# Rotary halves by a DVE shuffle instead of extra products, the next step's transpose moved into the attention, and ACT empties turned banks ahead of the exponentials

## The chip, the cores and the metric

The program runs on one core of a Trainium2 chip. The metric is the time of one execution on the device in microseconds (us); lower is better. All data are float32.

## The reference, cut to what matters

A decoder on a batch of 4 sequences of 512 positions, width 128, with a context of 154 positions. Four groups of layers follow one another, with self attention, cross attention and feed-forward parts of different kinds. The change bears on the second group's four layers of rotary attention most:

```python
DEPTH, HEADS, DH, ROT = 4, 8, 64, 32
def apply_rope(t, freqs):
    t1, tp = (t[..., :rot], t[..., rot:])            # rot = 32 of the 64 features of a head
    rh = jnp.concatenate([-t1[..., d2:], t1[..., :d2]], axis=-1)   # d2 = 16
    t1 = t1 * jnp.cos(freqs) + rh * jnp.sin(freqs)
    return jnp.concatenate([t1, tp], axis=-1)
def attn_block(xq, ctx, Wq, Wk, Wv, Wo, bo, pe_q, pe_k, mask):
    q, k, v = heads(xq @ Wq), heads(ctx @ Wk), heads(ctx @ Wv)
    q, k = apply_rope(q * DH ** (-0.5), pe_q), apply_rope(k, pe_k)
    sim = jnp.einsum('bhid,bhjd->bhij', q, k)        # masked in the self attention
    out = jnp.einsum('bhij,bhjd->bhid', jax.nn.softmax(sim, axis=-1), v)
    return out @ Wo + bo
# a layer: x += attn(rms(x)); x += attn(rms(x), context); x += gelu(rms(x) @ W1 + b1) @ W2 + b2
```

## The kernel before

**Order of the work.** A loop runs twice, once for each pair of sequences; the two sequences of a pair are lanes A and B. `ORDER` lists the steps (kind 5 is rotary self attention, 6 rotary cross attention, 7 the feed-forward step; kinds 5, 6, 7 occur for four layers), and each step runs for lane A and then for lane B. So there are 16 rotary self steps and 16 rotary cross steps in one execution. Each engine (PE, ACT, DVE, POOL) has one instruction stream; the streams meet only in semaphores (`self.r...`). Besides its own work a step carries parts of its neighbours: `prev.tail` on DVE adds the output of the step before to X, `nxt.head` computes the root-mean-square norm of the step after (the other lane, so it doesn't depend on this step), with one `pow` on POOL, and `nxt.pe_head`/`nxt.act_head` transpose that step's normed X on PE into a PSUM bank `XB` (`ps_O1`) and copy it to `XT` on ACT.

**A rotary step** (`L1Attention`; `L1Cross` is the same class with the context's 154 keys) makes four chunks of two heads each for K and Q, transposed: features on the partitions, positions along the row. The 32-partition blocks of a chunk hold, for each of two heads, first the 32 rotated features and then the 32 plain ones; `sin` is zero on the plain ones and carries the minus sign. For each K or Q chunk (index j) PE makes two products: one with the weights (`wq`, `wk`), one with weights whose halves were exchanged on the host (`swapq`, `swapk`). They go round a ring of four PSUM banks (`RING`: P0, P1, O0, O1). DVE multiplies the one by `cos` into Q or K and the other by `sin` into `part` (in `wide`), and POOL adds the two (line 1526). `order` is K of all four chunks, then Q of all four. Then the attention starts. The values of V are made inside it, in step 1 (`fill`, `fill2`).

**The attention** (`Attention`, used by seven kinds of step). It proceeds in steps i. In step i PE makes the scores of round i (line 515, four banks: S0, S1, OUT, T; places k = 0..3), every so many rounds it transposes the spread reciprocals (line 528), then transposes the exponentials of round i-1 (line 546) into rotating banks `PP3` (P0, P1, O0; two banks in the step `L0Moe`), and multiplies the transposed probabilities of round i-2 by V (line 564). DVE takes maxima (line 662), or adds the mask and takes them (line 658), and ACT takes the exponentials (line 633). The transposed banks are emptied ("turned") into `wide`: places 0 and 3 by ACT (line 588), 1 and 2 by DVE (line 590); ACT also empties the bank of the reciprocals into `RS` (line 597). PE may write a bank only when its use three banks before has been emptied. The ACT stream of a step before the change is, for each place k: exponential (i, k), then after k = 0 the reciprocals, then turn (i-1, k). Without an added mask the scores of round i+1 at place k wait for the exponential (i, k), which read the bank; with an added mask they wait for DVE alone.

A rotary self step has 8 rounds (two a chunk), a rotary cross step 4 (one a chunk, two blocks of queries at each place). `project` (line 693) multiplies by Wo at the end.

Of the kernel before, what the change touches and what calls it, by code (L numbers as in the profile page):

```python
# [129 lines left out]
class Table:  # L130


    def __init__(self, rows, before=None):
# [4 lines left out]
        for r in rows:  # L138
            if r[3] == "A":
                a += 1  # L140
            else:
                d += 1
            self.count.append((r[3], a if r[3] == "A" else d))
# [20 lines left out]
class Step:  # L164
# [17 lines left out]

    def beside(self, dve, *which):
# [10 lines left out]
def build(nc, io):  # L194
    ctx = ExitStack()
    with ctx:
# [12 lines left out]
        consts = sb("consts", [P, nconsts])  # L209
        lora_bias = sb("lora_bias", [P, 4])  # L210
# [130 lines left out]

        def evacuate(eng, r, tab, who, lo=0, hi=None):
            for j, row in enumerate(tab.rows[lo:hi], lo):
                if row[3] != who:
                    continue
# [89 lines left out]
        class Attention:  # L435
# [3 lines left out]
            def __init__(self, heads, dh, nkeys, added=None, causal=False, keys=None, queries=None,  # L439
                         banks=None, split="ADDA", exes=None):  # L440
# [15 lines left out]
                self.seq, self.first = [], []  # L456
                done = {"A": 0, "D": 0}
                self.recip_at = []
                for rd in range(self.rounds + 1):
# [5 lines left out]
                    for k in range(4 if rd < self.rounds else 0):  # L465
                        done[split[k]] += 1
                        self.seq.append((split[k], done[split[k]]))

# [25 lines left out]
            def evacuated(self, eng, r, s):  # L494
                e, n = self.seq[s]
                eng.wait_ge(r.turned_act if e == "A" else r.turned_dve, n)

            def pe(self, pe, r, ready=(), beside=None, wo=None, fill=None, fill2=None, valued=()):
                nb = len(self.banks)
                for i in range(self.steps):  # L500
                    if i == 1 and fill:
                        fill(pe)
# [17 lines left out]
                    if i == 1 and fill2:  # L520
                        fill2(pe)
# [30 lines left out]
                    if 0 <= rd < self.rounds:  # L552
# [14 lines left out]
                        ins.then_inc(r.av, 1)  # L567
                    if beside:
# [41 lines left out]
            def pool(self, pool, r):  # L610
                for rd in range(self.rounds):
                    self.spread(pool, r, rd)

            def act(self, act, r, free=None, fill=None):
                for i in range(self.steps):
                    if i == 1 and fill:
                        fill(act)
                    for k in range(4):
                        if i < self.rounds:
# [17 lines left out]
                        if k == 0 and i >= 2 and (i - 1) % self.rpc == 0:  # L637
# [4 lines left out]
            def dve(self, dve, r, free=None, beside=None):  # L642
                for i in range(self.steps):
                    for k in range(4):
# [56 lines left out]
        class LaneStep(Step):  # L701
# [35 lines left out]
            def pe_head(self, pe):  # L737
# [11 lines left out]
            def act_head(self, act):  # L749
# [128 lines left out]
        class Store(Step):  # L878
# [14 lines left out]
            def pe_head(self, pe):  # L893
                pass

            def act_head(self, act):
# [587 lines left out]
        class L1Attention(RootMeanSquare):  # L1484
            cross = False
            kind = 5

            def __init__(self, *a):
# [10 lines left out]
                self.part = [wide[:, 2048 + SEQ * j:2048 + SEQ * (j + 1)] for j in range(4)]  # L1499
                values = [([(src[:, c * kc:(c + 1) * kc], w("wv"))], kc, SEQ, "A", "copy",  # L1500
                           v_rows(kc, 8, 64, 64, c), None) for c in range(nch)]
                self.tab = Table([row for j in range(8) for row in self.rotary(j)])
                self.values = Table(values, self.tab)

            def dest(self, m, c):
                return QT[:, c, :] if m == "q" else KT[:, c, 0:self.NK]

            def rotary(self, j):
                m, c = self.order[j]
                n = SEQ if m == "q" else self.NK  # L1510
                x = self.L.XT[:, :] if m == "q" else self.src[:, :]
                by = (lambda t: ("times", (0.125, t))) if m == "q" else (lambda t: ("row", (t, ALU.mult)))
# [946 lines left out]
```

## Time and profile before

| | |
|---|---|
| time, median of 3 runs | 4449.32 us (4441.46 to 4451.9) |
| the profiled execution's own time | 4439.93 us |
| its span, first to last instruction | 4437.0 us |
| PE busy | 4059.2 us, 91% |
| DVE busy | 2674.6 us, 60% |
| ACT busy | 1998.3 us, 45% |
| POOL busy | 861.7 us, 19% |
| mean granted TensorE clock | 0.982 |

The busy times are averages over very different stages; whether an engine bounds a stage is read from the order of time there. A float32 matmul shows as two records, so "x4" on line 339 is two products. Where operations are pipelined their spans overlap by some 0.1 us, so the time that one costs is from start to start.

### The profile page before, as it was taken

What the parts mean: (1) busy time and instruction counts of PE and PEld (TensorE: products, weight loads), DVE (VectorE), ACT (ScalarE), POOL (GpSimd) and SP (SyncE); (2) the same over time, 40 slices, a digit from 0 to 9 for tenths busy, and PEclk for the clock granted to TensorE, in tenths of its full rate; (3) what the DMA queues carried; (4) which work ended last, traced back from release to release, by engine and by line L of the source; (5) the groups of instructions that cost most, each with busy time, mean ns of one, the idle gap of its engine ahead of it and who ended that gap; (6) DMA issues with size and microseconds to landing.
All of it is one profiled execution on the core that took longest, in us unless ns stands there. A gap on an engine that the chain in (4) does not pass through costs nothing. (4 is left out here: it accounts for less than half of the span.)

```text
span 4437.0 us, 71100 instructions
## 1 busy us (share of the span) xinstructions
PE 4059.2 (91%) x24156; PEld 2465.6 (56%) x24156; DVE 2674.6 (60%) x7163; ACT 1998.3 (45%) x5804; POOL 861.7 (19%) x972
## 2 busy tenths in 40 slices
PE   7988899999999998889989988999999999988899
PEld 4644456555556555555646444565555566555555
DVE  4687576666666645654446785766666666456544
ACT  2731445455445434663227313554554454346632
POOL 2146222112221200000020462222112212000000
PEclk9999999999999999999999999999999999999999
DMA  2000000000000010010010000000000000100000
GB/s 88 5 16 1 16 7 17 22 17 22 16 22 1 25 55 20 14 51 9 4 59 17 1 1 22 1 16 22 17 22 16 22 2 24 55 20 37 27 9 10
DMA packets 15849, 91.87 MB, mean 21 GB/s; under 512 B 2176, under 2 KB 8064, under 8 KB 12032
## 3 DMA queue, kind: packets, MB, share of 16 engines
q1 hardware_dynamic: 15488, 87.27, 5.4%
q8 instruction: 200, 3.28, 0.3%
q14 instruction: 161, 1.32, 0.1%
HBM read 86.22 MB, written 1.05 MB: 20 GB/s over the span
## 5 line engine op out<-in xcount | busy, mean ns | idle before, releaser
L564 PE MATMUL ps_O<-wide,V 128*64 128x256 f32 (+4 forms) x5152 | 597.1, 394 | 1.9 <-ACT wide L588 1.8
L633 ACT ACTIVATE EX<-NB,neg 128x154 f32<-128x154 f32 (+3 forms) x640 | 350.2, 551 | 399.8 <-DVE neg L658 399.7
L606 POOL COPY RX<-recips 128x256 f32<-128x256 f32 (+2 forms) x356 | 156.8, 440 | 1818.0 <-DVE recips L673 1754.4
L684 DVE TENSOR_TENSOR QT<-ps_O,RS 128x512 f32<-128x512 f32 x212 | 146.6, 692 | 444.8 <-PE ps_O L564 442.7
L588 ACT ACTIVATE wide<-ps_P 128x512 f32<-128x512 f32 (+2 forms) x648 | 367.6, 569 | 60.6 <-PE ps_P L546 60.5
L546 PE MATMUL ps_P<-consts,EX 128*128 128x128 f32 (+1 forms) x2148 | 316.4, 281 | 77.5 <-ACT wide L588 40.2
L399 POOL TENSOR_TENSOR small<-small 128x4 f32<-128x4 f32 x112 | 113.5, 1014 | 1407.3 <-DVE small L384 895.9
L515 PE MATMUL ps_S<-KT,QT 64*128 64x154 f32 (+7 forms) x1936 | 363.2, 458 | 25.7 <-issue 14.6
L564 PEld LDWEIGHTS ps_O<-wide,V 128*64 128x64 f32 (+4 forms) x5152 | 267.5, 128 | 195.6 <-issue 112.6
L515 PE MATMUL ps_OUT<-KT,QT 64*128 64x154 f32 (+5 forms) x968 | 331.5, 436 | 0.4 <-ACT EX L633 0.4
L590 DVE COPY wide<-ps_P 128x512 f32<-128x512 f32 (+4 forms) x404 | 259.4, 643 | 115.6 <-PE ps_P L546 115.0
L515 PE MATMUL ps_T<-KT,QT 64*128 64x154 f32 (+5 forms) x968 | 318.4, 430 | 4.5 <-ACT QT L633 3.3
L546 PEld LDWEIGHTS ps_P<-consts,EX 128*128 128x128 f32 (+1 forms) x2148 | 242.8, 146 | 134.7 <-ACT QT L633 54.7
L633 ACT ACTIVATE QT<-NB,neg 128x512 f32<-128x512 f32 (+1 forms) x384 | 259.4, 681 | 114.3 <-DVE neg L658 114.3
L546 PE MATMUL ps_P<-consts,QT 128*128 128x128 f32 (+1 forms) x1800 | 271.6, 281 | 31.1 <-ACT wide L588 31.1
L658 DVE CUSTOM_DVE_ANT_0 NB<-ps_S,maskb 128x512 f32<-128x512 f32 x256 | 166.6, 689 | 168.9 <-PE ps_S L515 168.9
L546 PEld LDWEIGHTS ps_P<-consts,QT 128*128 128x128 f32 (+1 forms) x1800 | 197.4, 143 | 123.3 <-issue 64.3
L515 PEld LDWEIGHTS ps_S<-KT,QT 64*128 64x128 f32 (+2 forms) x1936 | 152.3, 189 | 193.5 <-issue 159.5
L339 PE MATMUL ps_P<-XT,weights 128*128 128x512 f32 x512 | 246.0, 598 | 10.9 <-ACT XT L752 9.2
L339 PE MATMUL ps_O<-XT,weights 128*128 128x512 f32 (+1 forms) x472 | 223.9, 596 | 5.7 <-DVE KT L367 5.7
L633 ACT ACTIVATE EX<-ps_S,neg 128x154 f32<-128x154 f32 (+1 forms) x232 | 99.8, 440 | 237.6 <-DVE neg L662 237.2
L515 PEld LDWEIGHTS ps_OUT<-KT,QT 64*128 64x128 f32 (+2 forms) x968 | 157.4, 189 | 81.7 <-issue 74.9
(353 smaller groups left out, 8211.7 us busy)
## 6 DMA issues: line engine op xcount, KB each, us to landing
weights<-in_w_dram SPq DMA_DIRECT2D x10, 1664.0 KB, 6.8
weights<-in_w_dram SPq DMA_DIRECT2D x2, 6148.0 KB, 17.0
weights<-in_w5next_dram SPq DMA_DIRECT2D x6, 1664.0 KB, 6.9
weights<-in_w_dram SPq DMA_DIRECT2D x2, 4200.0 KB, 12.3
weights<-in_reltab_dram SPq DMA_DIRECT2D x2, 4096.0 KB, 13.4
weights<-in_w_dram SPq DMA_DIRECT2D x8, 640.0 KB, 3.9
weights<-in_w_dram SPq DMA_DIRECT2D x5, 832.0 KB, 4.3
weights<-in_w_dram SPq DMA_DIRECT2D x2, 2050.0 KB, 7.8
```

Source lines behind the costliest of these rows:

```text
L339: ins = pe.matmul(bank[0:row[1], 0:row[2]], lhsT, rhs, start=(i == 0), stop=(i == len(mms) - 1))
L399: pool.tensor_tensor(small[:, 36:40], small[:, 32:36], small[:, half:half + 4], ALU.pow).then_inc(r.rstd, 1)
L515: ins = pe.matmul(S4[k][:, a * N:(a + 1) * N], QT[strip, c, qts[a] * P:(qts[a] + 1) * P], self.keys(c)[strip, 0:N], start=True, stop=True)
L546: ins = pe.transpose(self.banks[s % nb][0:self.kc, b * P:(b + 1) * P], ex[:, a * N + kc * self.kc:a * N + (kc + 1) * self.kc], ident)
L564: ins = pe.matmul(O1[self.slot * j:self.slot * (j + 1), q0 * P:(q0 + self.nq) * P], self.value(c * self.hpc + j, kc), self.probs(rd, j)[:, ...
L588: eng.activation(dst, src, ACT.Copy).then_inc(r.turned_act, 1)
L590: eng.tensor_copy(dst, src).then_inc(r.turned_dve, 1)
L606: pool.tensor_copy(RX[:, q0 * P:(q0 + self.nq) * P].rearrange("p (n s) -> p n s", s=self.slot), of.unsqueeze(2).broadcast_to([P, self.nq * ...
L633: ins = act.activation(ex[:, a * N:(a + 1) * N], src, ACT.Exp, bias=neg[:, at:at + 1], scale=-1.0 if self.added else 1.0, accum_out=sums[: ...
L658: ins = dve.tensor_tensor_reduce(NB[:, k, a * N:(a + 1) * N], S4[k][:, a * N:(a + 1) * N], self.added(h, qt), -1.0, HUGE, ALU.add, ALU.min ...
L684: dve.tensor_tensor(self.out_chunk(c), O1[:, :], RS[:, c % 2, :], ALU.mult).then_inc(r.av_sb, 1)
```

## The change

It has three parts.

1. **Rotation.** The products with the swapped weights are gone (the weights are still loaded). The function `rope` reads the bank of the plain product twice on DVE: `stream_shuffle` with the list `HALVES` exchanges the halves of each block of 32 partitions into `part`, and a second operation multiplies the bank by `cos`. A third multiplies `part` by `sin` (`sinq`, made once at the start, holds 0.125 sin for the queries). In the cross step DVE does this third one for all eight chunks. In the self step DVE does it for the first two and POOL for the other six. POOL adds as before (`rotate`).
2. **Order.** K and Q chunks alternate (k0, q0, k1, q1, ...). Only four are made ahead of the attention, together with the values; the other four products and the transpose of the next step's X ("X") are made at the ends of steps of the attention, into the rotating banks (`late`: self step {1: [4], 2: [5, X], 3: [6], 4: [7]}, cross step {0: [4, 5], 1: [6, 7], 2: [X]}). DVE turns such a product at the start of its next step, ahead of the maxima. The head's second part (the norm itself) moves behind step 1 of the attention on DVE. PE no longer starts a cross step's K products before `XT` is there, and DVE does the tail ahead of them.
3. **ACT's order**, in every attention of the kernel: in steps that have something to turn, the reciprocals and turn (i-1, k) come ahead of exponential (i, k).

```diff
+        HALVES = [(m + 16) % 32 for m in range(32)]
+        def rope(dve, r, bank, dst, part, scale, wait, j, sin):
+            n = dst.shape[-1]
+            if wait:
+                dve.wait_ge(*wait)
+            dve.stream_shuffle(part, bank, HALVES).then_inc(r.evac_dve, 1)
+            if scale is None:
+                dve.tensor_tensor(dst, bank, K("cos")[:, 0:n], ALU.mult).then_inc(r.evac_dve, 1)
+            else:
+                dve.scalar_tensor_tensor(dst, bank, scale, K("cos")[:, 0:n], ALU.mult, ALU.mult).then_inc(r.evac_dve, 1)
+            if sin is not None:
+                dve.wait_ge(r.evac_dve, 2 * j + 1)
+                dve.tensor_tensor(part, part, sin, ALU.mult).then_inc(r.sum_step, 1)
...
             def pe(...):
+                    for j in self.late.get(i, ()):
+                        if self.late_at[j] >= nb:
+                            self.evacuated(pe, r, self.late_at[j] - nb)
+                        late(pe, j)
...
             def act(...):
+                    turn_first = 1 <= i <= self.rounds
                     for k in range(4):
+                        if turn_first:
+                            if k == 0 and i >= 2 and (i - 1) % self.rpc == 0:
+                                self.turn_recips(act, r, (i - 1) // self.rpc - 1)
+                            self.turn(act, r, "A", i - 1, k, free)
                         if i < self.rounds:
...
-                        if 1 <= i <= self.rounds:
+                        if 1 <= i <= self.rounds and not turn_first:
                             self.turn(act, r, "A", i - 1, k, free)
...
             def dve(...):
+                    for j in self.late.get(i - 1, ()):
+                        if j != "X":
+                            late(dve, j)
...
         class L1Attention
-                self.order = [("k", c) for c in range(4)] + [("q", c) for c in range(4)]
+                self.order = [(m, c) for c in range(4) for m in "kq"]
-                                     queries=lambda c: (self.r.rotated, 4 + c + 1))
+                                     queries=lambda c: (self.r.rotated, 2 * c + 2),
+                                     late={0: [4, 5], 1: [6, 7], 2: ["X"]} if cross else {1: [4], 2: [5, "X"], 3: [6], 4: [7]})
+                self.front = Table(ropes + values if cross else ropes[0:2] + values + ropes[2:4])
...
+            def rotate(self, pool, j):
+                r, d, part = self.r, self.dest(j), self.part(j)
+                pool.wait_ge(r.evac_dve, 2 * j + 2)
+                if not self.cross and j >= 2:
+                    pool.tensor_tensor(part, part, self.sines(j), ALU.mult).then_inc(r.sum_step, 1)
+                pool.wait_ge(r.sum_step, j + 1)
+                pool.tensor_tensor(d, d, part, ALU.add).then_inc(r.rotated, 1)
...
             def dve(self, dve):
+                parts = self.parts()
+                parts[0][0](dve, parts[0][1])
+                evacuate(dve, r, self.front, "D", 0, 2)
+                parts[1][0](dve, parts[1][1])
+                evacuate(dve, r, self.front, "D", 2)
```

## Rows read from the trace of the kernel before

**Rows 1.** The page: busy time of the engines.
```profile
PE 4059.2 (91%) x24156; PEld 2465.6 (56%) x24156; DVE 2674.6 (60%) x7163; ACT 1998.3 (45%) x5804; POOL 861.7 (19%) x972
```
**Rows 2.** Timeline of PE, self step, lane A: start us, us, operation, idle before.
```profile
1053.28 1.96 PE L339 MATMUL ps_P<-XT,weights 128*128 128x512 f32 x4 [0.78 <-ACT XT L752]
...
1058.50 1.88 PE L339 MATMUL ps_O<-XT,weights 128*128 128x512 f32 x4
1060.22 1.88 PE L339 MATMUL ps_P<-XT,weights 128*128 128x512 f32 x4
...
1067.80 1.13 PE L515 MATMUL ps_S<-KT,QT 64*128 64x512 f32 x4
...
1084.24 1.13 PE L515 MATMUL ps_S<-KT,QT 64*128 64x512 f32 x4
```
**Rows 3.** Windows: busy us of each engine, steps 3 on of that self attention.
```profile
1078.00:1124.00 46.00, 46.00 (x335) 29.61 (x336) 28.43 (x77) 29.00 (x73) 2.80 (x7) 1.00 0.01 1
```
**Rows 4.** Timeline of DVE, same step: two products turned, maxima, a late idle.
```profile
1064.11 0.68 DVE L365 SCALAR_TENSOR_TENSOR QT<-ps_O,consts 128x512 f32<-128x512 f32 x1
1064.71 0.68 DVE L365 SCALAR_TENSOR_TENSOR wide<-ps_O,consts 128x512 f32<-128x512 f32 x1
...
1097.46 0.69 DVE L658 CUSTOM_DVE_ANT_0 NB<-ps_S,maskb 128x512 f32<-128x512 f32 x1 [1.99 <-PE ps_S L515]
```
**Rows 5.** Timeline of PE, cross step of lane A and of lane B.
```profile
1195.96 0.69 PE L339 MATMUL ps_P<-CT,weights 128*128 128x154 f32 x4
1196.48 0.69 PE L339 MATMUL ps_O<-CT,weights 128*128 128x154 f32 x4
...
1209.22 0.63 PE L743 MATMUL ps_O<-consts,XN 128*128 128x128 f32 x4 [2.51 <-DVE wide L365]
...
1222.64 0.80 PE L515 MATMUL ps_S<-KT,QT 64*128 64x154 f32 x8
...
1252.91 3.23 PE L339 MATMUL ps_P<-weights,CT 128*77 128x512 f32 x4
```
**Rows 6.** Timeline of DVE, cross step: short products turned, maxima.
```profile
1197.73 0.32 DVE L367 TENSOR_TENSOR wide<-ps_P,consts 128x154 f32<-128x154 f32 x1
1197.99 0.32 DVE L367 TENSOR_TENSOR KT<-ps_O,consts 128x154 f32<-128x154 f32 x1
...
1209.76 0.47 DVE L662 TENSOR_REDUCE neg<-ps_OUT 128x2 f32<-128x308 f32 x1
```
**Rows 7.** Timeline of DVE: the head's norm, in a feed-forward and a self step.
```profile
1039.55 1.14 DVE L415 SCALAR_TENSOR_TENSOR XN<-X,small,weights 128x128 f32<-128x128 f32 x4
...
1059.72 1.96 DVE L415 SCALAR_TENSOR_TENSOR XN<-X,small,weights 128x128 f32<-128x128 f32 x4
```
**Rows 8.** Timeline of POOL, self step and cross step.
```profile
1059.47 1.27 POOL L1526 TENSOR_TENSOR KT<-KT,wide 128x512 f32<-128x512 f32 x1 [0.44 <-DVE wide L367]
...
1201.25 1.91 POOL L1526 TENSOR_TENSOR KT<-KT,wide 128x154 f32<-128x154 f32 x4
```
**Rows 9.** Windows: granted clock (the 1.00 or 0.57) after the idle of cross step A and B.
```profile
1252.00:1256.00 4.00, 3.89 (x8) 0.57 0.01 4
1209.00:1213.00 4.00, 3.71 (x23) 1.00 0.01 4
```
**Rows 10.** Waits of PE, cross attention of the last group, one of its four instances (1904 to 1975).
```profile
PE ps_P L546 <- ACT RS L597: 4.6, 4, 1.2
PE ps_O L546 <- ACT RS L597: 2.4, 2, 1.2
```
**Rows 11.** Timeline of ACT, a round of the same.
```profile
1926.17 0.42 ACT L633 ACTIVATE EX<-NB,neg 128x154 f32<-128x154 f32 x1 [2.08 <-DVE neg L658]
...
1927.00 0.57 ACT L597 ACTIVATE RS<-ps_P 128x512 f32<-128x512 f32 x1
```
**Rows 12.** Waits of PE, self attention of the last group, one of four instances (1742 to 1816).
```profile
PE ps_P L546 <- ACT wide L588: 4.7, 8, 0.9
PE ps_O L546 <- ACT wide L588: 3.3, 5, 1.0
```

More of the change, by code:

```diff
@@ L142, in __init__ @@
                 d += 1
+                if r[4] == "rope":
+                    d += 1
             self.count.append((r[3], a if r[3] == "A" else d))
@@ L181, in ch, with parts @@
         return self.chain
+    def parts(self):
+        return [(self.prev.tail, n) for n in range(self.prev.tail_parts)] + \
+            [(self.nxt.head, n) for n in range(self.nxt.head_parts)]
     def beside(self, dve, *which):
@@ L567, in pe @@
                         ins.then_inc(r.av, 1)
+                    for j in self.late.get(i, ()):
+                        if self.late_at[j] >= nb:
+                            self.evacuated(pe, r, self.late_at[j] - nb)
+                        late(pe, j)
                     if beside:
@@ L1500, in __init__ @@
+                ropes = [([self.product(j)], P, self.size(j), "D", "rope", self.dest(j), self.turning(j)) for j in range(4)]
                 values = [([(src[:, c * kc:(c + 1) * kc], w("wv"))], kc, SEQ, "A", "copy",
                            v_rows(kc, 8, 64, 64, c), None) for c in range(nch)]
-                self.tab = Table([row for j in range(8) for row in self.rotary(j)])
-                self.values = Table(values, self.tab)
-            def dest(self, m, c):
-                return QT[:, c, :] if m == "q" else KT[:, c, 0:self.NK]
@@ new lines, in size, with dest, part, before @@
+            def size(self, j):
+                return SEQ if self.order[j][0] == "q" else self.NK
+            def dest(self, j):
+                m, c = self.order[j]
+                return QT[:, c, :] if m == "q" else KT[:, c, 0:self.NK]
+            def part(self, j):
+                if self.cross:
+                    return NB[:, j % 4, 0:self.size(j)]
+                return wide[:, 2048 + SEQ * j:2048 + SEQ * (j + 1)] if j < 4 else self.L.flatXN
+            def before(self, j):
+                if self.cross:
+                    return (self.r.rotated, j - 3) if j >= 4 else None
+                return (self.r.rotated, j) if j >= 5 else None
@@ new lines, in product, with sines, turning @@
+            def product(self, j):
+                m, c = self.order[j]
+                return self.w("w" + m)[:, c * P:(c + 1) * P], self.L.XT[:, :] if m == "q" else self.src[:, :]
+            def sines(self, j):
+                return (sinq if self.order[j][0] == "q" else K("sin"))[:, 0:self.size(j)]
+            def turning(self, j):
+                return (self.part(j), 0.125 if self.order[j][0] == "q" else None, self.before(j), j,
+                        self.sines(j) if self.cross or j < 2 else None)
@@ L1521, in pool @@
                 self.fresh(pool)
-                for j in range(8):
-                    m, c = self.order[j]
-                    d = self.dest(m, c)
-                    pool.wait_ge(r.evac_dve, 2 * j + 2)
-                    pool.tensor_tensor(d, d, self.part[j % 4][:, 0:SEQ if m == "q" else self.NK], ALU.add
-                                       ).then_inc(r.rotated, 1)
-                self.att.pool(pool, r)
+                self.rotate(pool, 0)
+                self.rotate(pool, 1)
+                self.prev.pool_tail(pool)
```

131 lines of the change are left out of this document (67 added, 64 removed).

## The prediction, written before the changed kernel ran

> **What bounds the kernel now.** I read the page first: PE is busy for 91% of the span, DVE for 60% [rows 1]. That is an average, so I went through the timeline of PE in one rotary self step and one rotary cross step, then DVE, ACT and POOL over the same stretch, then the waits of PE in the other attentions, because the change of ACT's order touches all of them.
>
> In the self step, PE makes sixteen products of K and Q back to back, 1.72 us for two [rows 2], so 0.86 us each, about 14 us with one small wait, and goes straight into the scores. From the third step on it never rests (46.0 busy of 46.0 us), while DVE and ACT are busy for 28 and 29 [rows 3], and DVE idles 2 us before some of its maxima [rows 4]. So the self step is bound by PE all through; a product less is its 0.86 us less, if nobody else becomes late. In the cross step a K product costs 0.26 us (0.52 for two) and PE then stands 2.51 us in front of the transpose of the next X, which waited for DVE to finish the last product with the sine [rows 5]. There DVE already has the last word ahead of the attention. In the last group's attentions PE stands in every round or nearly, for a bank that ACT has not emptied [rows 10, 12].
>
> **The profiled execution** took 4439.93 us for a span of 4437.0; the sum is made against 4439.9, and the median of the runs shown, 4449.3, lies 9.4 above it. I add that at the end.
>
> **Part 1 and 2, the self step (16 of them).** Removed from PE: eight products, 8 x 0.86 = 6.9 us, all on its path. The question is whether DVE can follow, because the whole start is now compressed. I count from T0, the start of the first product, up to the scores of step 3. Before, that was from 1053.28 to 1084.24, 30.96 us [rows 2].
> PE afterwards, up to there: 8 products (four of K and Q, four of V) 6.9, three rounds of scores at 1.9, two rounds of transposes at 2.0, one round of probabilities by V 1.9, two late products 1.7, X 0.5: 18.7 us.
> DVE afterwards, up to there: tail 0.7, two ropes of three operations and three of two, 12 x 0.60 = 7.2 (0.60 is the start to start of a product turned [rows 4]), the head's two parts 0.9 and 2.3, twelve maxima at 0.61 = 7.3, four turns 2.4, small ones 0.3: 21.1 us, plus 0.2 until the tail can start, 21.3. So in this stretch DVE overtakes PE, and PE meets it: the bank of product 4 is free only when DVE has done its rope, behind the head's norm. I put the scores of step 3 at T0 + 21.9. After it two products (1.7) are still to be made under rounds in which DVE has about 5.5 us of work against 6.9 of PE, which hides it (3.8 to 4.4 now, and 1.2 of rope). The gain is 31.0 - 21.9 - 1.7 = 7.3 us; times 16, 117 us. Bounds: 5.5 if DVE is one more operation or two behind all the way, 8 if PE meets nothing. What hides POOL: its two operations for a late chunk are 2 x 1.27 = 2.5 us [rows 8], ready some 4 us after the step begins and wanted at the next step's scores, 6 us on. Without that cover each us would be on PE's path.
>
> **The cross step (16).** Removed from PE: four products at 0.86 and four at 0.26, 4.5 us, and the 2.5 us stand [rows 5]. Added to DVE: one operation for each chunk, 4 x 0.60 and 4 x 0.26 [rows 4, 6], 3.4 us in all, with everything ahead of fewer maxima. PE up to the scores of step 3 needs only some 16 us. DVE needs: tail 0.7, eight ropes of three, 12 x 0.60 + 12 x 0.26 = 10.3, head 3.2, twelve maxima of two blocks at 0.39 = 4.7 [rows 6], four turns 2.4, small and waits on semaphores 0.9: 22.2 us. So here DVE is the bound from T0 to T0 + 22, and PE waits for it in pieces below 2 us.
> To that a contention is added. The norm of the head, an operation with two inputs in SBUF, takes 1.14 us for four beside a resting POOL and 1.96 us beside POOL's add [rows 7, 8], a loss of 0.8 us. The new sine operation (`part` by `sin`) has two SBUF inputs too, and the head's squares fall onto POOL's add of q0 (1.27 us). I charge 1.2 us once a step, since a K chunk's add is short (1.91 for four [rows 8]) and falls under the next chunk's two operations out of PSUM. The Trainium skill (GPSIMD Engine Reference, table of the memories, SBUF interfaces) says that POOL shares these with VectorE when that runs an instruction of two SBUF inputs; the trace agrees. By that rule each of the eight sine operations could wait out an add; by rows this would be 8 x 0.8 = 6.4 us instead of 1.2, and the cross step would gain nothing.
> So the scores of step 3 stand at T0 + 23.4, against 1222.64 - 1195.96 = 26.7 before [rows 5]; what follows is the same work. Gain 3.3 us; times 16, 53 us. Bounds: below -2 (the rule at full price), above 4.5 + 2.5 + 0.6 = 7.6.
> Behind the 2.5 us stand, the two V products in lane B took 3.23 us in a stretch of granted clock 0.57, against 1.7 for two products elsewhere [rows 2]; after the same stand in lane A the clock was 1.00 [rows 5, 9]: one stretch at 1.2 instead of 2.4 GHz, some 1.7 us, which I see in 5 of the 16 cross steps. Without that stand they may go (9 us gained), or the new small stands may bring others. I take 0 and keep 10 us for either side.
>
> **The price of the shuffle.** No row has one. The nearest is the same engine's read of the same bank into SBUF, 0.60 us; the farthest, POOL's 1.27 for this shape [rows 4, 8]. I take 0.60, as every DVE operation over a 128x512 bank here costs that, whatever it computes; nothing below it shows. At 1.27 the chain of self and cross step would be longer by about 5 and 5 shuffles, 0.67 each, 16 x 6.7 = 107 us less gain. The Trainium skill (VectorE: DVE Perf Modes, the perf-mode tier table) gives about 2400 ns for 2048 elements, by which an estimate for 512 is 0.60 us; and its microarchitecture page (Vector Engine (DVE) Microarchitecture Reference, the reshape front-end) has the permutation loaded by an instruction of its own. No run here shows that one; it would be one more small row ahead of each shuffle.
>
> **Part 3, ACT's order.** In the last cross attention (4 instances, added mask, 8 rounds) ACT's first exponentials wait for DVE until 1926.17 and the reciprocals' bank is emptied only at 1927.00 [rows 11]; PE stands 1.20 us in six rounds, 7.0 us an instance [rows 10]. With the turn first the bank is free when PE gets to it. ACT needs 8 x 0.41 + 3 x 0.48 = 4.7 us a round against 5.7 of PE, so nothing else gets late: 6.5 of 7.0, times 4, 26 us. In the last self attention (4 instances, 16 rounds) the waits for turned banks are 8.0 us an instance [rows 12], and those for the reciprocals' bank 2.7 more. ACT has about 11.8 us for four rounds, PE 12.2 of the 15.1 they last, so part of the stand returns as a wait for exponentials: I take 7 of 10.7, 28 us. In the first group's attentions without a mask the gain is nothing: scores of the next round wait for the exponential of this one at place 3, and that now ends 0.5 us later, which gives back the 0.3 us that PE stood for the turn. In the rotary steps the exponentials have slack of 3 us in the self step; in the cross step DVE is late anyhow.
>
> **Sum.** 117 + 53 + 26 + 28 = 224. 4439.9 - 224 = 4216, and 9.4 for the median: 4225 us.
>
> **The rivals.**
> *DVE is the bound everywhere.* The removed products come back as waits for ropes: 4 us a self step, 0 a cross step, 30 from part 3, 94 us in all: 4355. For it: by my own count DVE is ahead of PE in work in both starts (21.1 against 18.7, 22.2 against 16), and a mask load or a contention would add to the longer one. Against it: from step 3 of the self step PE has no rest and DVE 40% [rows 3].
> *The turn first makes exponentials late.* ACT now waits for a transpose before it may take an exponential that was ready. Where there is no mask, that closes a ring: exponential, scores, transpose, turn. Part 3 then gives nothing, and the 4 rounds of a cross step lose 0.5 us each, 32 us: gain 117 + 53 - 32 = 138, 4311. For it: ACT's rounds there are 4.8 us, the ring with scores and transposes 5.8, as long as PE's round. Against it: only four rounds, of which the first two are DVE's.
> *PE meets nothing.* 8 x 16 + 7.6 x 16 + 70 = 320 us: 4130. For it: DVE's and PE's sums nearly agree in the self step. Against it: the count of DVE in the cross step.
> *Slower than before.* The shuffle is far dearer than a copy. Its place is the start of all 32 rotary steps, with 5 shuffles on the chain in each. 224 us are gone when each costs 224 / 160 = 1.4 us more than 0.60; from 2.0 us on the kernel is slower, at 2.5 us by some 80 us: 4530. The nearest rows speak against it, but none is a shuffle.
>
> **Chances.** The forecast with its own range, 4165 to 4300: 0.66. DVE everywhere (above 4325): 0.13. Exponentials late (4300 to 4325): 0.07. PE meets nothing (below 4165): 0.10. Slower: 0.04. The range 4150 to 4315 leaves out the last, DVE everywhere, and part of the third. A difference within 0.2% (9 us) is what a measurement of this kernel can't tell from none; faster by more 0.94, within 0.02, slower 0.04.
>
> **What would show it.** PE's records at line 339's place fall by 2 x 16 x 8 + 2 x 16 x 8 = 512 (both kinds of step). A shuffle of 128x512 at 0.6 to 0.7 us. From the first product to the scores of step 3, a self step takes about 21.9 us instead of 31.0, a cross step 23.4 instead of 26.7. The 2.5 us waits for DVE ahead of the transpose of X are gone; in their place PE waits for ropes in pieces of 0.5 to 1.5 us in steps 1 and 2, more in the cross step. The waits for line 597 in the last cross attention are gone. DVE busy rises by some 16 x 3.4 us, POOL by 16 x 6 x 1.27 = 122. The prediction is wrong if shuffles are dear, if DVE's operations stretch beside POOL's 2.5 us pairs in the self step, or if the granted clock falls in the new pieces.

## The result, and the profile after

The kernel after takes 4263.8 us (median of 4, 4253.7 to 4267.1) against 4450.2 us (4441.5 to 4451.9) for the kernel before: ratio 0.9581, 95% interval 0.9561 to 0.9602. The time lies inside the predicted range and 39 us above the predicted value. Its profiled execution took 4263.09 us for a span of 4261.1.

The page's busy times, which answer to [rows 1]:
```profile
PE 3944.9 (93%) x23644; PEld 2415.2 (57%) x23644; DVE 2716.7 (64%) x7580; ACT 2011.2 (47%) x5804; POOL 986.7 (23%) x1068
```
PE has 512 records less, POOL 125 us more, as forecast. The price of the shuffle stands in the groups of DVE by shape (count, then busy us and mean ns of one):
```profile
L358 DVE STREAM_SHUFFLE XN<-ps_P 128x512 f32<-128x512 f32 x64 | 46.5, 726 | 0.0
L358 DVE STREAM_SHUFFLE NB<-ps_P 128x154 f32<-128x154 f32 x48 | 15.8, 329 | 0.0
L358 DVE LOAD_MASK_SELECT NB<-ps_P x96 | 1.3, 13 | 0.7
```
**The self step.** PE's timeline, lane A (answers to [rows 2]):
```profile
1022.17 1.95 PE L347 MATMUL ps_P<-XT,weights 128*128 128x512 f32 x4 [0.78 <-ACT XT L809]
...
1029.26 1.13 PE L559 MATMUL ps_S<-KT,QT 64*128 64x512 f32 x4
...
1031.85 1.73 PE L559 MATMUL ps_S<-KT,QT 64*128 64x512 f32 x4 [0.59 <-DVE neg L715]
...
1045.08 1.13 PE L559 MATMUL ps_S<-KT,QT 64*128 64x512 f32 x4
```
From the first product to the scores of step 3: 22.9 us (30.96 before, 21.9 forecast). Behind the wait of 0.59 us for a maximum the scores of round 1 take 1.73 us instead of 1.13. The clock is not the reason, as the window over them shows (busy us of each engine, then the granted clock, 1.00):
```profile
1031.85:1033.58 1.73, 1.73 (x5) 0.88 (x6) 1.73 (x7) 1.73 (x5) 1.73 (x2) 1.00 0.00 0
```
PE starts one product every 0.61 us there, and DVE's maxima of the round before, which free the banks, start every 0.61 us as well. DVE's timeline over the same start (answers to [rows 4]):
```profile
1023.32 0.01 DVE L358 LOAD_MASK_SELECT wide<-ps_P  x1 [1.63 <-PE ps_P L347]
1023.94 0.67 DVE L360 TENSOR_TENSOR KT<-ps_P,consts 128x512 f32<-128x512 f32 x1
1024.53 0.68 DVE L365 TENSOR_TENSOR wide<-wide,consts 128x512 f32<-128x512 f32 x1
1025.13 0.01 DVE L358 LOAD_MASK_SELECT wide<-ps_P  x1
1025.77 0.67 DVE L362 SCALAR_TENSOR_TENSOR QT<-ps_P,consts 128x512 f32<-128x512 f32 x1
...
1027.64 1.11 DVE L438 TENSOR_SCALAR small<-small 128x4 f32<-128x4 f32 x1
```
The mask load and the shuffle together take 0.62 us, from 1023.32 to 1023.94. The last row, four numbers a partition, takes 1.11 us: POOL's add of q0 runs from 1027.33 to 1028.73.

**The cross step.** PE's timeline, lane A (answers to [rows 5]):
```profile
1152.98 0.43 PE L347 MATMUL ps_P<-CT,weights 128*128 128x154 f32 x2
...
1158.07 0.80 PE L559 MATMUL ps_S<-KT,QT 64*128 64x154 f32 x8 [0.96 <-POOL QT L1614]
...
1159.91 0.53 PE L1601 MATMUL ps_P<-CT,weights 128*128 128x154 f32 x2 [0.53 <-DVE QT L362]
...
1161.91 1.40 PE L559 MATMUL ps_S<-KT,QT 64*128 64x154 f32 x8 [0.61 <-POOL QT L1614]
...
1176.29 0.79 PE L559 MATMUL ps_S<-KT,QT 64*128 64x154 f32 x8
```
23.3 us to the scores of step 3 (26.7 before, 23.4 forecast), and the stand of 2.5 us is gone. But this step is one of only two of the 16 with a stretch at 1.2 GHz, which the window shows as a mean clock of 0.57. The same rows of lane B, without one:
```profile
1164.00:1168.00 4.00, 3.99 (x21) 3.68 (x22) 2.69 (x7) 1.77 (x8) 1.82 (x2) 0.57 0.00 0
```
```profile
1192.45 0.43 PE L347 MATMUL ps_P<-CT,weights 128*128 128x154 f32 x2
...
1214.62 0.79 PE L559 MATMUL ps_S<-KT,QT 64*128 64x154 f32 x8
```
That is 22.2 us, 1.2 less than forecast.

**Where the time went, step by step.** The place at which DVE takes up a step's output (adds it to X, in most steps) marks the step's end in every trace. From one such mark to the next, summed over the steps of a kind (us; one profiled execution each; the experiments below are in the same table):

| | rotary self, 16 | rotary cross, 16 | first group's cross, 4 | last self, 4 | last cross, 4 | ratio to before |
|---|---|---|---|---|---|---|
| before | 1181.9 | 672.2 | 219.6 | 310.0 | 302.0 | 1 |
| after | 1072.4 | 615.0 | 250.0 | 299.5 | 273.0 | 0.9581 |
| e1 order undone | 1101.2 | 660.6 | 219.9 | 311.6 | 302.0 | 0.9798 (0.9741 to 0.9854) |
| e2 order alone | 1167.5 | 707.2 | 249.0 | 302.3 | 272.9 | 1.0011 (1.0001 to 1.0021) |
| e3 masked only | 1072.5 | 668.1 | 219.9 | 298.1 | 273.0 | 0.9665 (0.9640 to 0.9690) |
| e5 recips first | 1132.1 | 655.0 | 225.4 | 311.1 | 291.6 | 0.9846 (0.9827 to 0.9865) |
| e7 first group behind | 1072.3 | 616.5 | 219.8 | 296.6 | 273.0 | 0.9511 (0.9493 to 0.9529) |
| e4 head first | 1076.0 | 625.4 | 251.5 | 299.7 | 272.9 | 0.9627 (0.9611 to 0.9643) |
| e6 sum beside PSUM | 1072.3 | 601.1 | 245.8 | 299.1 | 273.0 | 0.9540 (0.9523 to 0.9557) |
| e9 shuffle twice | 1122.8 | 671.6 | 251.5 | 296.1 | 273.0 | 0.9818 (0.9801 to 0.9835) |
| e10 product more | 1075.8 | 621.0 | 248.8 | 296.3 | 273.0 | 0.9570 (0.9554 to 0.9585) |
| e11 all in front | 1173.9 | 738.2 | 247.7 | 299.4 | 272.9 | 1.0086 (1.0071 to 1.0102) |
| e8 both mended | 1072.5 | 599.6 | 219.8 | 297.8 | 273.0 | 0.9482 (0.9466 to 0.9497) |

After against before: -109.4, -57.1, +30.4, -10.5, -29.0, together -175.6 of the span's -175.9. One shift between the first two columns is of the marks alone. Before, PE made the K products of a cross step and DVE turned them ahead of the tail; now the tail comes first. These are the marks of the two cross steps of lane A shown above, before and after, to be held against their first products at 1195.96 and 1152.98:
```profile
1198.49 0.68 DVE L824 TENSOR_TENSOR X<-ps_OUT,X 128x512 f32<-128x512 f32 x1
```
```profile
1153.18 0.69 DVE L881 TENSOR_TENSOR X<-ps_OUT,X 128x512 f32<-128x512 f32 x1 [0.68 <-PE ps_OUT L750]
```
So 2.3 us of each pair's cross work stood in the column of the self steps before, and stand in that of the cross steps after, eight times in all. Counted from first product to first product, a self step gained 5.7 us on the average and a cross step 4.7, not 6.8 and 3.6. The one column with the other sign, the first group's unmasked cross attention, was forecast at nothing. Its rounds show the loss. PE and ACT in one of them, kernel after:
```profile
139.64 0.39 PE L559 MATMUL ps_T<-KT,QT 32*128 32x154 f32 x1 [0.69 <-ACT EX L687]
...
140.35 1.12 PE L570 MATMUL ps_O<-consts,RX 128*128 128x128 f32 x4
141.26 1.91 PE L588 MATMUL ps_P<-consts,EX 128*77 128x128 f32 x8
...
146.43 0.39 PE L559 MATMUL ps_T<-KT,QT 32*128 32x154 f32 x1 [0.58 <-ACT QT L687]
...
151.92 0.39 PE L559 MATMUL ps_T<-KT,QT 32*128 32x154 f32 x1 [0.69 <-ACT EX L687]
```
```profile
139.09 0.41 ACT L687 ACTIVATE EX<-ps_T,neg 128x154 f32<-128x154 f32 x1
...
141.51 0.60 ACT L643 ACTIVATE RS<-ps_O 128x512 f32<-128x512 f32 x1 [1.92 <-PE ps_O L570]
...
142.85 0.38 ACT L687 ACTIVATE QT<-ps_S,neg 128x154 f32<-128x154 f32 x1
```
PE's scores at place 3 (bank T) wait for the exponential of the round before; when they are done PE transposes, and only then may ACT, which stood 1.92 us, empty the bank and go on to exponentials that had been ready. Two rounds go from 139.64 to 151.92, 12.3 us. The same two rounds before took 9.8 us. The windows of the two rounds after, and of the two before, (busy us of each engine, then the granted clock) show that this is not the clock alone:
```profile
139.64:146.43 6.79, 6.21 (x52) 5.08 (x53) 3.72 (x8) 4.62 (x19) 0.40 (x1) 0.75 0.00 0
146.43:151.92 5.49, 4.78 (x49) 3.30 (x49) 2.94 (x7) 4.02 (x18) 0.40 (x1) 1.00 0.01 3
```
```profile
142.13:146.80 4.67, 4.35 (x48) 3.01 (x48) 3.23 (x8) 4.01 (x19) 0.40 (x1) 1.00 0.01 4
146.80:151.96 5.16, 4.82 (x52) 3.44 (x53) 3.44 (x8) 4.50 (x20) 0.40 (x1) 1.00 0.00 2
```
The round at clock 1.00 lasts 5.5 us, the next one, at 1.00 too, 6.0 (its window would end at 157.88); these two lengths alternate, 5.7 on the average, where 4.7 and 5.2 alternated before. By an estimate from these rows, 0.8 us more in each of some six rounds of four steps, about 20 of the 30.4 us are the order's directly. The clock takes part in the rest: added up from windows of 4 us, time at 1.2 GHz was 164 us before and 205 us after, and these four steps alone had some 44 us more of it.

### The profile page after: what moved, and what is told of

Same layout as the page of the kernel before. It is cut to its first block and busy times, and to the rows that moved or that the text cites. A ratio compares the mean times of both kernels' runs of the same rounds, so it can differ in the third digit from the quotient of the medians.

```text
span 4261.1 us, 70671 instructions
## 1 busy us (share of the span) xinstructions
PE 3944.9 (93%) x23644; PEld 2415.2 (57%) x23644; DVE 2716.7 (64%) x7580; ACT 2011.2 (47%) x5804; POOL 986.7 (23%) x1068
## 5 line engine op out<-in xcount | busy, mean ns | idle before, releaser
L559 PE MATMUL ps_S<-KT,QT 64*128 64x154 f32 (+7 forms) x1936 | 383.4, 463 | 59.1 <-POOL QT L1614 25.4
L636 DVE COPY wide<-ps_P 128x512 f32<-128x512 f32 (+4 forms) x484 | 311.0, 645 | 80.8 <-PE ps_P L588 79.3
L634 ACT ACTIVATE wide<-ps_P 128x512 f32<-128x512 f32 (+4 forms) x488 | 274.9, 564 | 149.2 <-PE ps_P L588 149.1
L559 PE MATMUL ps_T<-KT,QT 64*128 64x154 f32 (+5 forms) x968 | 325.8, 439 | 17.1 <-ACT EX L687 9.0
L588 PE MATMUL ps_P<-consts,EX 128*128 128x128 f32 (+1 forms) x1956 | 295.1, 285 | 30.2 <-ACT wide L634 17.6
L559 PEld LDWEIGHTS ps_S<-KT,QT 64*128 64x128 f32 (+2 forms) x1936 | 160.9, 189 | 252.2 <-issue 160.7
L588 PEld LDWEIGHTS ps_P<-consts,EX 128*128 128x128 f32 (+1 forms) x1956 | 228.1, 150 | 81.5 <-issue 45.7
L588 PE MATMUL ps_P<-consts,QT 128*128 128x128 f32 (+1 forms) x1672 | 254.2, 285 | 20.9 <-ACT wide L634 18.6
L634 ACT ACTIVATE wide<-ps_O 128x512 f32<-128x512 f32 (+3 forms) x256 | 145.7, 569 | 115.0 <-PE ps_O L588 115.0
L719 DVE TENSOR_REDUCE neg<-ps_S 128x2 f32<-128x308 f32 (+1 forms) x264 | 129.6, 531 | 107.0 <-PE ps_OUT L559 55.6
L750 PEld LDWEIGHTS ps_OUT<-weights,QT 128*128 128x128 f32 x1536 | 178.3, 192 | 24.8 <-issue 24.8
```

The source lines that it names most:

```text
L559: ins = pe.matmul(S4[k][:, a * N:(a + 1) * N], QT[strip, c, qts[a] * P:(qts[a] + 1) * P], self.keys(c)[strip, 0:N], start=True, stop=True)
L588: ins = pe.transpose(self.banks[s % nb][0:self.kc, b * P:(b + 1) * P], ex[:, a * N + kc * self.kc:a * N + (kc + 1) * self.kc], ident)
L634: eng.activation(dst, src, ACT.Copy).then_inc(r.turned_act, 1)
L636: eng.tensor_copy(dst, src).then_inc(r.turned_dve, 1)
L719: ins = dve.tensor_reduce(neg[:, at:at + self.w], S4[k][:, 0:self.w * N].rearrange("p (a k) -> p a k", k=N), AX.X, ALU.max, negate=True)
L750: ins = pe.matmul(OUT[:, t * P:(t + 1) * P], self.out_chunk(c)[:, t * P:(t + 1) * P], wo[:, c * P:(c + 1) * P], start=(c + t == 0), stop=( ...
```

## The experiments

**e1: ACT's order undone.** In `Attention.act`:
```diff
-                    turn_first = 1 <= i <= self.rounds
+                    turn_first = False
```


> The kernel after, with the turn behind the exponential again in every attention step (part 3 of the change undone, parts 1 and 2 kept). Ring theory: where scores wait for an exponential (no mask), the turn first closes a ring and costs, elsewhere it gives. Then the four unmasked cross attentions of the first group get their 30 us back, the last cross attention gives back its 29.0 us (1.20 us waits of PE in six rounds return), the last self attention 10.5, the rotary steps stay within 0.5 us each (their start is DVE's): 4264 - 30 + 29 + 10 = 4273, between 4260 and 4290. Rival, clock and not order: the first group's loss of 30 us comes from stretches at 1.2 GHz that have nothing to do with the order; it stays, and the time is 4303. By the prediction's own step (nothing lost there, 54 gained) it would be 4318.

Measured 4353.4 us, ratio 0.9798: 2.3% slower than after, by far more than all three numbers foresaw. Its runs lie further apart than those of the other kernels, from 4328.8 to 4383.4 us, all of them slower than every run of after. The first and last groups' cross attentions did what the ring theory said (219.9, 302.0). The miss is in the rotary steps, which lost 28.8 and 45.6 us. Each of the 16 rotary cross steps now has one more wait of PE:
```profile
960.83 0.63 PE L588 MATMUL ps_O<-consts,QT 128*77 128x128 f32 x4 [1.73 <-ACT RS L643]
```
and ACT shows why, in the same round:
```profile
959.35 0.39 ACT L687 ACTIVATE EX<-ps_S,neg 128x154 f32<-128x154 f32 x1 [3.10 <-DVE neg L719]
...
960.09 0.59 ACT L643 ACTIVATE RS<-ps_O 128x512 f32<-128x512 f32 x1
```
ACT stood 3.10 us in front of an exponential whose maximum DVE had not made, with the full bank queued behind it. With the ropes in front of the maxima DVE is late, and the old order hands this lateness on to PE. In the self step the same is a wait of 1.31 us for a turned bank. A cross step without a stretch at 1.2 GHz takes 40.25 us instead of 38.29, which makes 31 of the 45.6 us; the other 14 came with some 31 us more time at 1.2 GHz in these steps.

**e2: ACT's order alone**, the kernel before with `act` of after.

> The kernel before, with only the turn put ahead of the exponential (part 3 alone). Ring theory: +30 us in the first group's cross attentions, -29 in the last cross attention, -10 in the last self attention, and in the rotary steps, whose rounds PE bounds, between 0 and +1 us each: 4450 - 9, up to 4455 if the unmasked rotary rounds lose 0.5 us a step. By the prediction's step (54 us gained) 4396. Rival, the gain of the last group hangs on the shuffle's shift: nothing changes there, and the time is above 4470.

Measured 4446.7 us, ratio 1.0011: no gain. First and last groups as in after; the rotary self steps gained 14.4 us, the rotary cross steps lost 35.0. In the self steps the one wait of 0.66 us for a turned bank, which the kernel before had in each, is gone. In the cross steps the scores at place 3 wait for an exponential, 0.69 us where it was 0.21; at clock 1.00 the last two rounds take 6.2 and 6.0 us instead of 5.0 and 5.7. Stretches at 1.2 GHz came as well (245 us in all against 164, 34 of them more in the cross steps), and the 35.0 us are both together. So with the products of before, the turn first closes the ring in the rotary cross step too.

**e3: turn first only where a mask is added.**
```diff
+                    turn_first = self.added is not None and 1 <= i <= self.rounds
```


> The kernel after, with the turn first only in attentions that add a mask (rotary self, last self, last cross), and the exponential first where there is none (first group's attentions, rotary cross, second group's). Ring theory: the 30 us of the first group's cross attentions come back and nothing of the last group's 39 is lost: 4234. If the rotary cross step's ring also loses 0.5 us in its later rounds, 8 to 16 us more: down to 4220. Rival, clock and not order: 4264 within 5 us.

Measured 4292.7 us, ratio 0.9665, slower than after. The 30 us came back, and the rotary cross steps lost 53. The expectation that they would gain was wrong, for the reason of e1: without a stretch at 1.2 GHz they take the 40.25 us of e1, which makes 31 us, and the rest came with 55 us more time at 1.2 GHz in them.

**e5: only the reciprocals' bank first**, turns behind the exponential.

> The kernel after, with only the bank of reciprocals emptied ahead of the exponential, and the four turns behind it as in the kernel before. Theory A, the reciprocals' bank is what PE lacked in the cross attentions: the last cross attention keeps its 29 us, the rotary cross step loses its one stand of 1.7 us for RS and stays near the 38.3 us of the kernel after (with everything behind it was 40.25), the rotary self step goes back to 67.1 to 68.6 (its stand of 1.3 us is for a turn), 29 us in all, and the first group's cross attentions, whose ring is closed by the turn, get 20 to 30 us back: 4264 + 29 - 25 = 4268, ratio to before 0.960. Rival, the turns of the same place are what counts: rotary cross 40.25, last cross attention back at 76.8, together 60 us more: 4320, ratio 0.972.

Measured 4378.8 us, ratio 0.9846, worse than both theories said, and no better than e1. Theory A falls: the last cross attention kept 10.4 of its 29.0 us. PE's wait for RS is gone there and one for the turned bank, 0.66 us in most rounds, stands in its place. The rotary self steps lost 59.7 us, more than with everything behind: waits of 0.56 us for the bank of line 634 come in rounds that had none. A half of the reordering only moves the wait one bank on.

**e7: the old order in the first group's cross attention alone.** `turn_first = not self.behind and ...`, and `behind=True` in that step.

> The kernel after, with the old order (turn behind the exponential) in the first group's cross attention alone. Ring theory: its 4 instances get 30 us back and nothing else moves: 4264 - 30 = 4234, ratio 0.951. Rival, what was won there is lost to another state of the TensorE clock in the steps behind it, as in the masked-only kernel, whose rotary cross steps had stretches at 1.2 GHz: ratio 0.955 or more.

Measured 4232.3 us, ratio 0.9511 as expected. The rival falls; time at 1.2 GHz is 161 us, that of the kernel before. So the 30 us are the order's.

**e9: a second shuffle.**
```diff
+            dve.stream_shuffle(spare, bank, HALVES)
             dve.stream_shuffle(part, bank, HALVES).then_inc(r.evac_dve, 1)
```


> The kernel after, with a second shuffle of every bank into a spare buffer ahead of the real one (256 shuffles more, 0.62 us each for 512 columns and 0.23 for 154; nothing reads them). Theory, DVE bounds the start of both rotary steps: each step pays its shuffles on the chain at full price, eight in the cross step (3.4 us) and five in the self step (3.1 us), 16 x 6.5 = 104 us: 4368, ratio 0.982. Rival, PE and POOL bound it and DVE has slack: less than half, 4310 or less.

Measured 4367.8 us, ratio 0.9818, as expected. A self step grew by 3.0 us where the clock stayed at 1.00 (3.1 expected): there DVE's operations at the start are on the path at full price. A cross step grew by 3.54 (3.4 expected), but this is not shown to be the shuffles' price alone: all 16 now have stretches at 1.2 GHz, 92 us of them against 7 in after. The shortest grew by 3.2 us, with one stretch; in after one stretch went with 1.2 us. By an estimate from these numbers the shuffles themselves cost between 2.0 and 3.2 us of the 3.4 there, still more than the half that the rival allowed.

**e10: an idle product more.** `idle(pe, S[0], 1)` behind the front's products.

> The kernel after, with one idle product of 128x512 (0.86 us of PE) behind the front's products in both rotary steps; nothing reads it. Theory, DVE and POOL bound the start: in the cross step it falls into PE's stand of 0.97 us for POOL's add and costs 0 to 0.1; in the self step PE's only stand before step 3 is 0.6 us, so it costs 0.3 to 0.4: 16 x 0.35 = 6 us, ratio 0.960. Rival, PE bounds both: 0.86 each, 28 us, ratio 0.964. In its trace the stand for POOL in the cross step should shrink to 0.1.

Measured 4263.0 us, ratio 0.9570, the same as after. A cross step without a stretch at 1.2 GHz took 38.26 us (38.29 in after; with one some 1.2 us more), a self step 0.18 more than in after. Of PE's two stands for POOL's adds in the cross step the first, 0.97 us, is gone, filled by the product; the second, 0.62 us, is still there. PE does not bound the start of either step.

**e11: all eight chunks ahead of the scores**, all sines on DVE, POOL only adding:
```diff
-  late={0: [4, 5], 1: [6, 7], 2: ["X"]} if cross else {1: [4], 2: [5, "X"], 3: [6], 4: [7]})
+  late={2: ["X"]})
-                         self.sines(j) if self.cross or j < 2 else None)
+                         self.sines(j))
```


> The kernel after, with all eight shuffled chunks made ahead of the scores, as before made its sixteen products, all sines on DVE, and POOL only adding (the late chunks of the change undone; shuffle and ACT's order kept). Theory, DVE bounds the start and the late chunks are what turns the saved products into time: in the self step three ropes and three sines more come before the scores of step 3, 3 x 1.8 + 3 x 0.6 = 7.2 us, less 1.7 us of late products and what DVE catches up, so +4.5 a step, 70 us; in the cross step all eight ropes lay ahead of step 3 anyhow, +0 to 1.5: together 4264 + 70 + 12 = 4346, ratio 0.977. Rival, the saved products alone pay: within 15 us of the kernel after, ratio 0.961 or less.

Measured 4491.0 us, ratio 1.0086, slower than the kernel before, though PE makes 256 products less than it did. I expected 0.977. A self step lost 6.3 us against after (4.5 expected), a cross step 7.7 (0 to 1.5 expected). PE in a self step and in a cross step:
```profile
1101.06 2.68 PE L559 MATMUL ps_S<-KT,QT 64*128 64x512 f32 x4 [6.15 <-DVE neg L715]
```
```profile
1241.04 1.79 PE L559 MATMUL ps_S<-KT,QT 64*128 64x154 f32 x7 [3.04 <-POOL QT L1610]
```
What I had missed for the cross step: DVE's sum up to step 3 is the same, but with all ropes ahead of the first maxima ACT and PE have nothing to do meanwhile, and afterwards DVE waits for them (the columns are as above; DVE's idle time stands in brackets):
```profile
1242.62 0.98 DVE L719 TENSOR_REDUCE neg<-ps_S 128x2 f32<-128x308 f32 x2 [1.46 <-PE ps_S L559]
...
1246.52 0.69 DVE L636 COPY wide<-ps_P 77x512 f32<-77x512 f32 x1 [1.83 <-PE ps_P L588]
```
Time at 1.2 GHz rose to 461 us. How much of the loss is the clock's and how much the waits' these runs do not part. In the self step the edit also moves six sines from POOL to DVE, so the late chunks are undone by themselves only in the cross step.

**e4 and e6: the contention with POOL.** e4 puts the head's squares ahead of the first two ropes:
```diff
                 parts[0][0](dve, parts[0][1])
+                if self.prev.tail_parts == 1:
+                    parts[1][0](dve, parts[1][1])
                 evacuate(dve, r, self.front, "D", 0, 2)
```
e6 puts the shuffles and cosines of chunk 1 beside POOL's add of q0, then the squares, then the two sines:
```diff
+                if self.cross:
+                    evacuate(dve, r, self.front, "D", 2)
+                    parts[1][0](dve, parts[1][1])
+                    sine(dve, r, self.part(2), 2, self.sines(2))
+                    sine(dve, r, self.part(3), 3, self.sines(3))
```


> The kernel after, with the head's squares of the next X ahead of the first two ropes (where the step before has one tail part) instead of behind them, so that they no longer run beside POOL's add of q0; the same instructions otherwise. Contention theory: the small scaling behind the squares takes 0.17 us instead of 1.11, DVE bounds the start, and each of some 30 rotary steps ends 0.9 us earlier: 4264 - 27 = 4237. Rival, the wait for q0 bounds the start: the first ropes come 0.8 us later, the scores of step 0 with them, and the time stays at 4264 or rises by up to 30 x 0.8 = 24 us.

> The kernel after, in the rotary cross step with the shuffles and cosines of chunk 1 straight behind those of chunk 0 (they read PSUM), then the head's squares, then the two sine products. So POOL's add of q0 runs beside PSUM reads only. Contention theory: no instruction of DVE is stretched to 1.1 or 1.2 us there, and each of 16 cross steps ends 0.9 us earlier: 4264 - 14 = 4250 (ratio 0.955). Rival, PE's wait for POOL's add bounds the start: the second round's scores wait for q1 0.6 us as before, and the time stays (ratio 0.958).

e4 measured 4279.7 us, ratio 0.9627, slower than after; e6 4241.9, ratio 0.9540, faster. In e4 the small scaling does take 0.17 us, but its loss went to the next operation that met POOL's add, the short sine product:
```profile
940.18 1.20 DVE L365 TENSOR_TENSOR NB<-NB,consts 128x154 f32<-128x154 f32 x1
```
That it came out slower than after has another part too: with the squares moved ahead, DVE stands for those that ACT makes:
```profile
937.13 0.17 DVE L438 TENSOR_SCALAR small<-small 128x4 f32<-128x4 f32 x1 [0.29 <-ACT XN L855]
```
In e6 neither meets it (0.17 and 0.31 us):
```profile
931.63 0.17 DVE L443 TENSOR_SCALAR small<-small 128x4 f32<-128x4 f32 x1
931.71 0.31 DVE L370 TENSOR_TENSOR NB<-NB,consts 128x154 f32<-128x154 f32 x1
```
and a cross step without a stretch at 1.2 GHz takes 37.3 us instead of 38.3. From DVE's first shuffle to its first maximum the same operations take 5.6 us instead of 6.6, 0.94 us less, which is what the scaling alone had been stretched by. So the contention cost 0.97 us on the path of the cross step, once a step, and moving one of its victims does not remove it. Of the gain of e6 the columns give 13.9 us to the steps that it edits.

**e8: e6 and e7 together.**

> The kernel after with both edits that paid alone: the old order in the first group's cross attention (ratio to before 0.9511 alone), and the sine products of chunk 1 behind the head's squares in the rotary cross step (0.9540 alone). The kernel after stood at 0.9581. They lie in different steps, so they should add up: 0.9581 - 0.0070 - 0.0041 = 0.947, about 4213 us. Rival, clock stretches that move with every shift eat some of it: 0.950 or more.

Measured 4217.4 us (4214.4 to 4229.8), ratio 0.9482 (0.947 expected), 1.0% faster than after. Both gains are there (599.6 and 219.8).

## Why the prediction was right, and where it was not

- **The self step**, 7.3 us forecast, 6.84 measured by the marks (109.4 / 16), 5.7 from first product to first product: the term was too large by 1.6. DVE overtakes PE at the start as said (e9, e10); the start came out 1.0 us longer. The scaling of 1.11 us, which I had charged to the cross step alone, stands on DVE here too, but that it is the reason is not shown: in e4 it took 0.17 us here too, and the self steps did not get shorter (1076.0 against 1072.4). My sum of PE's work up to step 3 was added wrongly: its terms give 20.7 us, not 18.7. DVE's 21.1 are still more, so the forecast of the start, which goes by DVE, does not change, but "DVE is ahead of PE" rested on 0.4 us and not on 2.4.
- **The cross step**, 3.3 forecast, 3.57 measured by the marks, 4.7 from first product to first product: too small by 1.4. That self and cross step together came out within 4 us of the 170 forecast is luck, two errors of opposite sign. The start came out 1.2 us shorter than counted, 22.2 instead of 23.4 us, though DVE did meet POOL; the 23.3 of lane A agrees only through its stretch at 1.2 GHz. And the kernel before had such stretches in 10 of its 16 cross steps, not in the 5 that I had seen, 34 us in all, of which 7 are left; at half speed that is, by an estimate, up to 14 us gained, which I had taken as 0. I charged 1.2 us for one meeting with POOL; e6 makes it 0.97. By the rule at full price all eight sines would meet an add. They do not: each add is issued by the sine before it and runs beside the next chunk's two PSUM reads or the maxima, so the victim is the first small operation behind q0. The Trainium skill (SBUF — State Buffer, "Who interferes with whom") says of `tensor_scalar` that it may take the pair shared with GpSimd, and that operations with two SBUF inputs contend too. The traces agree for both, 1.11 us instead of 0.17 and 1.20 instead of 0.31.
- **The shuffle's price**, 0.60 taken, 0.62 from start to start; 0.23 for 154 columns. The mask load costs 0.01 to 0.02 us. The slower rival had no ground.
- **ACT's order in the last cross attention**, 26 forecast, 29.0 measured. PE's waits for RS fell from 27.9 to 3.6 us in the four instances, those for turned banks from 6.1 to 3.1.
- **In the last self attention**, 28 forecast, 10.5 measured. The term was mis-sized: in one instance PE's waits for emptied banks fell from 10.7 to 3.4 us, as forecast, but its length only from 76.7 to 73.7. From the starts of PE's products the scores took 17.1 us instead of 13.9 in that instance, with as much time at 1.2 GHz in both; the products of the other lines took what they had taken. So about half of the stand came back inside the scores and not as a wait for exponentials. New waits for maxima before PE's weight loads (3.9 us of about 60 us, 1.8 before) point to DVE; this was not tested.
- **In the first group's cross attention**, nothing forecast, 30.4 us lost. This is the step that failed. I wrote that the exponential's 0.5 us would be given back by the 0.3 us that PE stood for the turn, a sum of two small times, where it is a ring: exponential, scores at place 3, transpose, turn, exponential. A ring is charged its whole length a round, 5.7 us at clock 1.00 against the 4.9 that a round took. I had that mechanism as a rival, with a ring of 5.8 us, but priced it only in the rotary cross step.
- **In the rotary steps** I gave the order no worth, and named the ring as the danger. With the shuffle it is worth 28.8 us in the self and 45.6 us in the cross steps (e1), 14 of these with the clock. The parts are not a sum: shuffle and late chunks with the old order give 80.7 + 11.6 = 92.3 us there, the order alone loses 35.0 - 14.4 = 20.6, both together give 166.5. My count of 7.3 and 3.3 us followed DVE's chain alone; as far as e1 shows, that holds only when ACT does not pass DVE's lateness on to PE. Why the ring does not bite in the changed cross step, while with the products of before the order cost 35.0 us, the clock's part included (e2), is argued and not shown: there DVE's ropes make the first rounds longer than the ring.
- **The clock**, 0 taken with 10 us for either side: 41 us more at 1.2 GHz. They are a balance: some 44 us more in the first group's cross attentions, which e7 takes away, 10 and 7 more in the last self and rotary self steps, 27 less in the rotary cross steps.
- **The rivals.** "DVE is the bound everywhere" is what e11 shows: with the late chunks undone, and in the self step all sines on DVE, the saved products are worth nothing. That the change escapes it is the work of the late chunks, no less than of the shuffle; in the cross step, where e11 changes nothing else, they are worth 7.7 us a step, the clock's part included.
- **The whole.** 224 forecast, 175.9 measured on the span; the terms, by the marks, missed by -30.4, -17.5, -7.6, +4.1 and +3.0, which is all of it.

## What to carry to other kernels

Taking work from the busiest engine pays only if the engine that inherits the start is given its work in pieces between the others' rounds: here the kernel with half the chunks late was 4.2% faster than before, and the one with all of them in front 0.9% slower. Before an in-order engine's queue is changed, ask for each attention which of the two heads of the queue comes late: put the one that is late behind, and if the two feed each other through a third engine, count the ring's length against the round.

## What was not expected of the hardware

- A DVE scaling of four numbers a partition took 1.11 us instead of 0.17 beside POOL's addition of 128x512, while shuffles and cosines out of PSUM kept 0.6 us from start to start beside the same addition. In e4 the loss moved to a product of two SBUF operands of 154 columns, 1.20 us instead of 0.31.
- The instruction that loads the shuffle's mask took 0.01 to 0.02 us; shuffles of 512 columns cost as much as a copy.
- An idle product of 0.86 us in each of 32 steps cost nothing measurable in all (e10 against after: 0.9570 and 0.9581); at clock 1.00 a self step grew by 0.18 us and a cross step not at all.
